# One block for the context's last rows, the heads and the attention of a perceiver layer, with statistics taken tile by tile

## The chip, the cores and the metric

The kernel runs on one core of a Trainium2 chip. The metric is the device time of one execution in microseconds; the time before is the median of three runs. The profile shows one execution with its engines: TensorE (PE, its weight loads PEld), VectorE (DVE), ScalarE (ACT), GpSimd (POOL) and SyncE (SP), which here only issues DMAs.

## The reference, cut to what matters

The input x is 32 x 32 tokens of 512 values, the context 32 batches of 257 rows of 128. A layer is a cross attention, a Mamba-like mixer with an MLP, and a mixture of experts. The change lies in the cross attention, the first 390 of 1021 us:

```python
q_hk = (hidden_q @ Wq.T).reshape(b, s, H, K)          # hidden_q: the layer norm of x; H = 16, K = 128
q_big = jnp.einsum('bshk,hkq->bshq', q_hk, w_kc_q)
kv_rope = kv_c * cos[None] + _rotate_half(kv_c) * sin[None]
q_r = jnp.einsum('bshq,hqr->bhsr', q_big, W_qr)
k_r = jnp.einsum('bld,hdr->bhlr', kv_rope, W_kr)
...
```

Softmax of q_r with k_r over the 257 rows weights the rotated context, which goes through w_kc_kv and Wo and is added to x. The kernel folds the weights of a head into small products first (N = w_kc_q and W_qr, A = Wq and N, G = w_kc_kv and Wo).

## The kernel before, in words

Every matmul of full precision is three passes of a high and a low part (`passes`, L43 to L45). High parts are copies by ScalarE, low parts subtractions by VectorE. Each engine has its own program, in order; semaphores carry the dependencies. A `Block` holds one program for each engine, and at its end all engines wait for each other.

The first block (`phase_context_tail`, L77 to L113) loads row 257 of each context batch, two small tables, the identity and the eight 128-token tiles of x (L93); VectorE rotates the rows (L101 to L105), TensorE transposes them (L113), VectorE keeps the result (L107), SP stores the rows (L96).

The second block (`phase_heads`) is the heads stage. `Norm` does the layer norm: `statistics` (L147, bn_stats of four tiles, then four bn_aggr and a sum, twice), `roots` on POOL (L144), `rows` (L162), and for each tile four transposes (`transpose_tile`, L177), a high part (L182) and a low part (L168), in three PSUM banks taken in turn. `fold_n` (L459) and `fold_a` (L470) prepare the weights of the first pair of heads between them. Then come eight passes, each of two heads. A pass has `features` for the first half of the tokens (12 matmuls of 512 columns), `fold_n` of the next pass, `turn_context` (L512, transposes of a rotated context), `features` for the second half, another turned context, `fold_a` of the next, `queries` (L501), `fold_g` (L479), and two more of each. `keep_n` (L620) and `split_a` (A_lo at L624, k_lo at L627) are VectorE's part of the folding, A_hi (L545) and k_hi (L547) ScalarE's.

POOL rotates one context batch after the other (L379 to L388, five operations), four batches to a pass. It needs the sine and cosine tables, the raw context, the tail rows of that batch in a broadcast load, and a place in x: the cosine table and one raw buffer lie in tile 3 of x, the tails in tile 2, the rotated batches in tiles 4 to 7, so SP loads the cosine table and all contexts only behind `sp.wait_ge(norm.normed, TT)` (L432), eight rows normalised. SP's queue is in order: a wait in it holds everything that is behind.

The third block (`phase_attention`) takes 32 batches in steps: `scores` (matmuls of 256 columns), maxima on VectorE (L953, L955), exponentials on ScalarE (L906), normalising on VectorE (L967) and POOL (L796), transposes (L839), the context product, and the output of a tile of tokens. The operands of its first two batches are made at the end of the heads stage (`first_columns` L646, `first_queries` L650, with the semaphores first_lo and first_q). SP loads later batches' operands from L752 and L757 on.

## Time and profile before

| | |
|---|---|
| three runs | 1024.33, 1026.26, 1026.9 us (median 1026.26) |
| the profiled execution | 1022.87 us, span 1021.1 us |
| TensorE's mean granted clock | 0.988 |
| first block, to the end of its barrier | 0 to about 7.2 us |
| heads stage | to about 137.4 us |
| attention stage | to about 390 us |

The span is what the engines' records cover; the execution's own time is 1.8 us longer. A row of the timeline gives the start in us, the time in us, the engine, the line, the operation with what it writes and reads, how many were merged into the row, and in brackets how long the engine had been idle before and what released it. A granted clock of 1.00 is 2.4 GHz, 0.50 is 1.2 GHz.

### The profile page before, as it was taken

What the parts mean: (1) busy time and instruction counts of PE and PEld (TensorE: products, weight loads), DVE (VectorE), ACT (ScalarE), POOL (GpSimd) and SP (SyncE); (2) the same over time, 40 slices, a digit from 0 to 9 for tenths busy, and PEclk for the clock granted to TensorE, in tenths of its full rate; (3) what the DMA queues carried; (4) which work ended last, traced back from release to release, by engine and by line L of the source; (5) the groups of instructions that cost most, each with busy time, mean ns of one, the idle gap of its engine ahead of it and who ended that gap; (6) DMA issues with size and microseconds to landing.
All of it is one profiled execution on the core that took longest, in us unless ns stands there. A gap on an engine that the chain in (4) does not pass through costs nothing. (4 is left out here: it accounts for less than half of the span.)

```text
span 1021.1 us, 15950 instructions
## 1 busy us (share of the span) xinstructions
PE 955.3 (94%) x5479; PEld 805.6 (79%) x5479; DVE 556.1 (54%) x1040; ACT 411.1 (40%) x954; POOL 453.3 (44%) x489
## 2 busy tenths in 40 slices
PE   4899976999999988999999999889999999999997
PEld 4677755888787866888888988677778899999997
DVE  6333468888899944444545332317968333333345
ACT  2333467677677734223432044352333122222111
POOL 1998845555576620000000302217614878993051
PEclk9999989999999999999999999999999999999999
DMA  6788702111111004422221014312023756661152
GB/s 221 231 269 264 225 13 93 35 40 42 32 37 38 27 27 130 139 83 82 82 89 36 3 59 138 102 29 81 2 85 113 262 171 235 202 225 63 42 159 99
DMA packets 79003, 109.91 MB, mean 108 GB/s; under 512 B 14224, under 2 KB 46992, under 8 KB 78928
## 3 DMA queue, kind: packets, MB, share of 16 engines
q1 hardware_dynamic: 66288, 82.18, 25.9%
q10 hardware_dynamic: 10080, 18.35, 5.0%
q0 software_dynamic: 2560, 8.39, 2.5%
q8 instruction: 45, 0.74, 0.3%
q14 instruction: 30, 0.25, 0.1%
HBM read 83.13 MB, written 25.77 MB: 107 GB/s over the span
## 5 line engine op out<-in xcount | busy, mean ns | idle before, releaser
L43 PE MATMUL psum<-second_xT_hi,second_w_hi 128*128 128x512 f32 x272 | 107.6, 396 | 7.0 <-DVE second_w_lo L1259 3.8
L45 PE MATMUL psum<-second_xT_hi,second_w_lo 128*128 128x512 f32 x272 | 106.6, 392 | 0.0
L44 PE MATMUL psum<-second_xT_lo,second_w_hi 128*128 128x512 f32 x272 | 106.5, 392 | 0.0
L1152 POOL TENSOR_TENSOR all_x<-all_x,mlp_raw 128x512 f32<-128x512 f32 x8 | 10.0, 1290 | 174.7 <-DVE all_x L1654 174.7
L2172 ACT ACTIVATE moe_s<-psum 128x352 f32<-128x352 f32 x39 | 18.1, 465 | 151.0 <-PE psum L45 151.0
L43 PEld LDWEIGHTS psum<-second_xT_hi,second_w_hi 128*128 128x128 f32 x272 | 51.4, 189 | 20.0 <-DVE second_w_lo L1259 5.3
L2238 DVE TENSOR_TENSOR moe_hT_lo<-psum,moe_hT_hi 128x384 fp32r<-128x384 f32 x39 | 21.8, 558 | 79.1 <-ACT moe_hT_hi L2178 79.1
L1609 ACT ACTIVATE mlp_s<-psum,mlp_side 128x512 f32<-128x512 f32 x32 | 21.8, 682 | 100.3 <-PE psum L45 100.3
L43 PE MATMUL psum<-moe_w_hi,moe_tT_hi 128*128 x184 | 61.3, 333 | 0.0
L1654 DVE TENSOR_TENSOR all_x<-all_x,psum 128x512 f32<-128x512 f32 x64 | 43.8, 687 | 31.7 <-PE psum L45 31.2
L45 PEld LDWEIGHTS psum<-second_xT_hi,second_w_lo 128*128 128x128 f32 x272 | 51.4, 189 | 11.0
L44 PEld LDWEIGHTS psum<-second_xT_lo,second_w_hi 128*128 128x128 f32 x272 | 51.5, 189 | 10.5
L45 PE MATMUL psum<-moe_w_hi,moe_tT_lo 128*128 x184 | 59.1, 321 | 0.0
L44 PE MATMUL psum<-moe_w_lo,moe_tT_hi 128*128 x184 | 58.9, 320 | 0.0
L43 PE MATMUL psum<-q_G_hi,att_cT_hi 128*128 128x512 f32 x128 | 53.3, 416 | 0.9 <-DVE all_x L985 0.9
L2019 POOL TENSOR_TENSOR moe_w_lo<-far_raw,moe_w_hi 128x1408 fp32r<-128x1408 f32 x16 | 51.6, 3226 | 0.0
L44 PE MATMUL psum<-q_G_lo,att_cT_hi 128*128 128x512 f32 x128 | 50.7, 396 | 0.0
L43 PE MATMUL psum<-moe_w_hi,moe_hT_hi 128*128 (+3 forms) x117 | 48.4, 414 | 2.2 <-DVE moe_hT_lo L2238 2.2
L1648 DVE TENSOR_TENSOR mix_wo_lo<-mlp_s,mix_wo_hi 128x512 fp32r<-128x512 f32 x32 | 22.1, 690 | 51.5 <-ACT mix_wo_hi L1615 51.5
L45 PE MATMUL psum<-mix_wo_hi,mix_wo_lo 128*128 128x512 f32 x128 | 49.9, 390 | 0.0
L43 PE MATMUL psum<-mix_wo_hi 128*128 128x512 f32 x128 | 49.9, 390 | 0.0
L44 PE MATMUL psum<-mix_wo_lo,mix_wo_hi 128*128 128x512 f32 x128 | 49.8, 389 | 0.0
(341 smaller groups left out, 2887.0 us busy)
## 6 DMA issues: line engine op xcount, KB each, us to landing
kv_all<-all_x ACTq DMA_DIRECT2D x28, 256.0 KB, 4.1
far_raw<-in_eg SPq DMA_DIRECT2D x10, 704.0 KB, 4.6
far_raw<-in_eu SPq DMA_DIRECT2D x10, 704.0 KB, 4.6
slot_rows<-mix_W SPq DMA_DIRECT2D x23, 256.0 KB, 5.9
slot_out<-far_rows ACTq DMA_DIRECT2D x23, 256.0 KB, 2.4
far_raw<-in_ed SPq DMA_DIRECT2D x10, 512.0 KB, 4.1
far_rows<-slot_rows ACTq DMA_DIRECT2D x19, 256.0 KB, 2.9
second_raw<-in_w_feat SPq DMA_DIRECT2D x18, 256.0 KB, 3.3
```

The source lines that it names most:

```text
L43: e.matmul(out, hi_l, hi_r, start=first, stop=False)
L44: e.matmul(out, hi_l, lo_r, start=False, stop=False)
L45: return e.matmul(out, lo_l, hi_r, start=False, stop=last)
L1152: pool.tensor_tensor(g["x"][:, t, :], g["x"][:, t, :], b2, ALU.add).then_inc(x_plus, 1)
L1609: act.activation(s1[:, m % 2, :], psum[:, UP + m % 4, :], ACT.Gelu_apprx_tanh, bias=side[:, p, c:c + 1]).then_inc(act_ok, 1)
L1648: v.tensor_tensor(h_lo[:, c, half * HALF:(half + 1) * HALF], s1[:, m % 2, :], h_hi[:, c, half * HALF:(half + 1) * HALF].bitcast(F32), ALU. ...
L1654: v.tensor_tensor(x[:, t, :], x[:, t, :], psum[:, DN + t % 4, :], ALU.add).then_inc(dn_ok, 1)
L2019: pool.tensor_tensor(w1_lo[:, u, i, :, :], raw1[:, i, :, :], w1_hi[:, u, i, :, :].bitcast(F32), ALU.subtract).then_inc(w_ok, 1)
L2172: act.activation(s[:], psum[:, GB + j % 2, 0:FE], ACT.Silu).then_inc(s_ok, 1)
L2238: v.tensor_tensor(hT_lo[:], psum[:, HB, 0:NC * P].rearrange("p (c k) -> p c k", k=P), hT_hi[:].bitcast(F32), ALU.subtract).then_inc(hlo_ok, 1)
```

## The change

The three blocks become one. `phase_heads` and `phase_attention` return their programs, and `phase_opening` puts one behind the other on every engine; the work of the first block goes to the front of the heads' programs, with its small tiles in the raw context buffers and the rotated row in `rows`. Where a block's end had ordered things, waits on semaphores stand: POOL and SP wait for `heads.rot` of all 32 batches, TensorE for first_q and first_lo of each of the first two batches and for all of G, ScalarE for kvT_ok, VectorE for kept. `statistics` is split into `tile_statistics` and `moments`. VectorE takes them as tiles land and normalises the first rows before the second half's statistics are complete. TensorE transposes tiles 4 to 6 between the groups of the first half's features and tile 7 behind them. SP issues the first two contexts and the tail store before it waits, the cosine table once four rows are normalised instead of eight; POOL waits for one more normalised row before each of its first four batches.

```diff
-def phase_context_tail(nc, d, g):
...
-    def statistics(self, v):
-        for half in range(2):
-            tiles = range(half * TT // 2, (half + 1) * TT // 2)
-            for t in tiles:
-                v.wait_ge(self.loaded[t], 16)
-                v.bn_stats(self.stats[:, t, :], self.g["x"][:, t, :]).then_inc(self.stat_done, 1)
-            for t in tiles:
-                v.wait_ge(self.stat_done, t + 1)
-                v.bn_aggr(self.mv[:, t, :], self.stats[:, t, :]).then_inc(self.aggr, 1)
-            v.wait_ge(self.aggr, (half + 1) * TT // 2)
-            these = slice(tiles[0], tiles[-1] + 1)
-            v.tensor_scalar(self.var[:, these, 0], self.mv[:, these, 1], EPS, None, ALU.add).then_inc(self.var_done, 1)
+    def tile_statistics(self, v, t):
+        v.wait_ge(self.loaded[t], 16)
+        v.bn_stats(self.stats[:, t, :], self.g["x"][:, t, :]).then_inc(self.stat_done, 1)
+
+    def moments(self, v, half):
+        tiles = range(half * TT // 2, (half + 1) * TT // 2)
+        for t in tiles:
+            v.wait_ge(self.stat_done, t + 1)
+            v.bn_aggr(self.mv[:, t, :], self.stats[:, t, :]).then_inc(self.aggr, 1)
+        v.wait_ge(self.aggr, (half + 1) * TT // 2)
+        these = slice(tiles[0], tiles[-1] + 1)
+        v.tensor_scalar(self.var[:, these, 0], self.mv[:, these, 1], EPS, None, ALU.add).then_inc(self.var_done, 1)
 
...
+
+        row, cosr, sinr, t2 = (raw[0:B, i, j, :] for i in range(2) for j in range(2))
+        turned = rows[0:B, 0:P]
...
         g["kv_out"] = kv_out
-        block = ctx.enter_context(nc.Block())
-
-        @block.gpsimd
-        def _(pool):
+        loaded, rotated, turned_T, kept = n.sem("loaded"), n.sem("rotated"), n.sem("turned_T"), n.sem("kept")
+
+        def gpsimd(pool):
             norm.roots(pool)
             pool.wait_ge(tables, 32)
+            pool.wait_ge(g["tail_stored"], 16)
             for b in range(B):
                 src, kvr = raws[b % RAW], kvx[:, b % KVB, 0, :, :]
                 pool.wait_ge(raw_in[b % RAW], 16 * (b // RAW + 1))
 
                 wait(pool, kv_out[b % KVB], 16 * (b // KVB))
+                if b < KVB:
+
+                    pool.wait_ge(norm.normed, TT - KVB + b + 1)
 
                 wait(pool, rot_sum, b)
                 pool.tensor_tensor(kvr, src, cosb[:], ALU.mult).then_inc(rot_mid, 1)
...
                     load_context(b + RAW)
                 if b % 2 == 1 and b + 3 < B:
                     load_tails((b + 3) // 2)
+            sp.dma_start(row, d["ctx"][:, L - 1, :]).then_inc(loaded, 16)
+            sp.dma_start(cosr, d["cos_last"]).then_inc(loaded, 16)
+            sp.dma_start(sinr, d["sin_last"]).then_inc(loaded, 16)
+            sp.dma_start(ident[:], d["ident"]).then_inc(loaded, 16)
+            for t in range(TT):
+                sp.dma_start(x[:, t, :], d["x"][t * P:(t + 1) * P, :]).then_inc(g["x_loaded"][t], 16)
             load_n(0)
             load_a(0)
+            sp.wait_ge(rotated, 4)
+            sp.dma_start(d["tail_rows"][:, :], turned).then_inc(g["tail_stored"], 16)
             sp.dma_start(sinb, d["sin_main"]).then_inc(tables, 16)
+            load_context(0)
+            load_context(1)
             load_g(0)
+            sp.wait_ge(norm.normed, TT - KVB)
+            sp.dma_start(cosb, d["cos_main"]).then_inc(tables, 16)
             sp.wait_ge(g["tail_stored"], 16)
+            load_tails(0)
+            load_context(2)
             load_n(1)
+            load_tails(1)
             load_a(1)
-            sp.wait_ge(norm.normed, TT)
-            sp.dma_start(cosb, d["cos_main"]).then_inc(tables, 16)
-            load_context(0)
-            load_tails(0)
-            load_context(1)
-            load_context(2)
-            load_tails(1)
             for p in range(NP):
                 contexts(BPP * p)
                 if p + 2 < NP:
...
                 for c in range(DC):
                     m = passes(pe, psum[:, RB + half, :], A_hi[:, c, :], A_lo[:, c, :], xT_hi[:, c, cols], xT_lo[:, c, cols],
                                c == 0, c == DC - 1)
+                    if p == 0 and half == 0 and c < DC - 1:
+                        norm.transpose_tile(pe, TT // NHALF + c)
                 m.then_inc(r_ready, 1)
+                if p == 0 and half == 0:
+                    norm.transpose_tile(pe, TT - 1)
 
             def queries(p, half):
                 pe.wait_ge(k_kept, p + 1)
...
                 for c in range(2):
                     m = pe.transpose(psum[:, KT, c * P:(c + 1) * P], kvx[:, b % KVB, 0, c, :], ident[:])
                 m.then_inc(kvT_ready, 1)
-            for t in range(3):
+            pe.wait_ge(rotated, 4)
+            pe.transpose(psum[:, NB, 0:B], turned, ident[0:B, 0:B]).then_inc(turned_T, 1)
+            pe.wait_ge(kept, 1)
+            for t in range(2):
                 norm.transpose_tile(pe, t)
             fold_n(0)
+            norm.transpose_tile(pe, 2)
+            fold_a(0)
             norm.transpose_tile(pe, 3)
-            norm.transpose_tile(pe, 4)
-            fold_a(0)
-            for t in range(5, TT):
-                norm.transpose_tile(pe, t)
             for p in range(NP):
                 features(p, 0)
                 if p + 1 < NP:
...
                 nb, h, half = HALF // S, 2 * p, 1 - half
                 act.activation(q[:, half * nb:(half + 1) * nb, h * S:(h + 1) * S],
                                psum[:, XB, :].rearrange("p (b s) -> p b s", s=S), ACT.Copy).then_inc(q_kept[0], 1)
-            for t in range(5):
+            for t in range(3):
                 norm.high_part(act, t)
             keep_a(0)
-            for t in range(5, TT):
+            for t in range(3, TT):
                 norm.high_part(act, t)
             for p in range(NP):
                 keep_features(p, 0)
...
                 v.wait_ge(first_q_hi, s + 1)
                 v.tensor_tensor(q_lo[:, s, :], q[:, place_of(s), :], q_hi[:, s, :].bitcast(F32), ALU.subtract).then_inc(first_q, 1)
 
-            norm.statistics(v)
-            v.wait_ge(g["tail_stored"], 16)
+            v.wait_ge(loaded, 64)
+            v.tensor_tensor(turned, row, cosr, ALU.mult).then_inc(rotated, 1)
+            v.tensor_tensor(t2[:, 0:64], row[:, 64:128], sinr[:, 0:64], ALU.mult).then_inc(rotated, 1)
+            v.tensor_tensor(t2[:, 64:128], row[:, 0:64], sinr[:, 64:128], ALU.mult).then_inc(rotated, 1)
+            v.wait_ge(rotated, 3)
+            v.tensor_tensor(turned, turned, t2, ALU.add).then_inc(rotated, 1)
             for t in range(4):
-                norm.rows(v, t)
-            for t in range(2):
-                norm.low_part(v, t)
-                norm.rows(v, 4 + t)
+                norm.tile_statistics(v, t)
+            norm.moments(v, 0)
+            v.wait_ge(turned_T, 1)
+            v.tensor_copy(g["tailT"][:], psum[:, NB, 0:B]).then_inc(kept, 1)
+            norm.tile_statistics(v, 4)
+            norm.tile_statistics(v, 5)
+            norm.rows(v, 0)
+            norm.rows(v, 1)
+            norm.tile_statistics(v, 6)
+            norm.tile_statistics(v, 7)
+            norm.moments(v, 1)
+            norm.rows(v, 2)
+            norm.rows(v, 3)
+            norm.low_part(v, 0)
+            norm.low_part(v, 1)
             keep_n(0)
-            for t in range(2, 4):
-                norm.low_part(v, t)
-                norm.rows(v, 4 + t)
-            norm.low_part(v, 4)
+            norm.low_part(v, 2)
+            norm.rows(v, 4)
+            norm.low_part(v, 3)
+            norm.rows(v, 5)
             split_a(0)
-            for t in range(5, TT):
+            norm.rows(v, 6)
+            norm.rows(v, 7)
+            for t in range(4, TT):
                 norm.low_part(v, t)
             for p in range(NP):
...
-        def _(sp):
+        def sync(sp):
             kv_out = g["kv_out"]
             KVB = len(kv_out)
+
+
+            sp.wait_ge(heads.rot, B)
...
                 of = pr(b)[:, 2:4, :]
                 pool.tensor_tensor(of, of, pair(scale, b, 1).unsqueeze(2).to_broadcast([P, 2, LM]), ALU.mult).then_inc(pr_far_ok, 1)
 
+            pool.wait_ge(heads.rot, B)
             pool.memset(g["power"][:], -0.5).then_inc(power_set, 1)
...
                     columns_lo(s + 2)
                     queries_lo(s + 2)
 
-        @block.tensor
-        def _(pe):
+        def tensor(pe):
             def scores(b):
                 p = b % 2
-                wait(pe, q_ok, b + 1 - DONE)
-                wait(pe, kvT_ok, b + 1 - DONE)
+                if b < DONE:
+                    pe.wait_ge(heads.first_q, b + 1)
+                    pe.wait_ge(heads.first_lo, b + 1)
+                else:
+                    pe.wait_ge(q_ok, b + 1 - DONE)
+                    pe.wait_ge(kvT_ok, b + 1 - DONE)
                 if b - 2 in EARLY:
 
...
 
-            def output(t, heads):
-                if heads[0] == 0:
+            def output(t, heads_now):
+                if heads_now[0] == 0:
+                    if t == 0:
+                        pe.wait_ge(heads.g_kept, H)
                     pe.wait_ge(c_ok, BPT * (t + 1))
...
+            act.wait_ge(heads.kvT_ok, B)
             for s in range(B + 2 + BPT):
...
+            v.wait_ge(heads.kept, 1)
...
+    made.gpsimd, made.sync, made.tensor, made.scalar, made.vector = gpsimd, sync, tensor, scalar, vector
+    return made
+
+
+def phase_opening(nc, heads, attention):
+    with nc.Block() as block:
+
+        @block.gpsimd
+        def _(pool):
+            heads.gpsimd(pool)
+            attention.gpsimd(pool)
+
+        @block.sync
+        def _(sp):
+            heads.sync(sp)
...
```

## Rows read from the trace of the kernel before

**Rows 1.** The page, part 1: busy time, share, instructions of each engine.
```profile
PE 955.3 (94%) x5479; PEld 805.6 (79%) x5479; DVE 556.1 (54%) x1040; ACT 411.1 (40%) x954; POOL 453.3 (44%) x489
```

**Rows 2.** Table by stage: stretch, length, busy of each engine, PEclk, DMA share, GB/s.
```profile
39.42:122.46 83.04, 81.10 (x460) 61.31 (x458) 31.46 (x54) 33.52 (x72) 75.71 (x127) 1.00 0.84 257
137.44:260.00 122.56, 108.02 (x617) 93.33 (x618) 103.84 (x224) 86.36 (x287) 66.74 (x74) 0.96 0.16 48
```

**Rows 3.** Timeline of the opening, VectorE: the first four statistics.
```profile
7.23 2.47 DVE L152 BATCH_NORM_STATS2 all_stats<-all_x 128x6 f32<-128x512 f32 x4 [1.82 <-PEq L79]
```

**Rows 4.** Line L93 (min/median/max); DMA issues from 9.65 to 10 us, time to landing.
```profile
L93 SPq DMA_DIRECT2D all_x<-in_x x8: 432/432/437, 2.6 to 5.9; - x8
DMA to landing us min/median/max: 2.7/4.3/5.2
...
heads_wkr<-in_wkrT SPq DMA_DIRECT2D x1, 64.0 KB, 5.0
```

**Rows 5.** Timeline of the opening: POOL's root, VectorE, ScalarE.
```profile
10.34 1.05 POOL L144 TENSOR_TENSOR heads_rstd<-heads_var,heads_power 128x4 f32<-128x4 f32 x1 [3.04 <-DVE heads_var L158]
...
12.97 1.91 DVE L162 TENSOR_SCALAR queries_q<-all_x,heads_mv,heads_rstd 128x512 f32<-128x512 f32 x4
...
18.38 0.29 DVE L620 COPY queries_q<-psum 128x128 f32<-128x128 f32 x1 [0.83 <-PE psum L459]
...
19.64 0.68 DVE L168 TENSOR_TENSOR first_xT_lo<-psum,first_xT_hi 128x512 fp32r<-128x512 f32 x1
...
20.99 0.60 ACT L545 ACTIVATE heads_A_hi<-psum 128x512 fp32r<-128x512 f32 x1 [1.08 <-PE psum L470]
21.49 0.30 ACT L547 ACTIVATE heads_k_hi<-heads_wkr 128x128 fp32r<-128x128 f32 x1
21.62 0.69 DVE L624 TENSOR_TENSOR heads_A_lo<-psum,heads_A_hi 128x512 fp32r<-128x512 f32 x1 [0.25 <-ACT heads_A_hi L545]
```

**Rows 6.** Timeline of the opening, TensorE.
```profile
13.57 2.82 PE L177 MATMUL psum<-all_ident,queries_q 128*128 128x128 f32 x12 [8.39 <-DVE queries_q L162]
16.19 2.15 PE L459 MATMUL psum<-queries_q,heads_kcqT 128*128 128x64 f32 x12
18.18 1.04 PE L177 MATMUL psum<-all_ident,queries_q 128*128 128x128 f32 x8
19.06 1.90 PE L470 MATMUL psum<-queries_q,heads_wq 128*128 128x64 f32 x16
```

**Rows 7.** Timeline of the first pass, TensorE and POOL's first rotation.
```profile
22.37 0.50 PE L43 MATMUL psum<-first_xT_hi,heads_A_hi 128*128 128x512 f32 x1
...
25.28 1.45 PE L459 MATMUL psum<-queries_q,heads_kcqT 128*128 128x64 f32 x12
...
26.20 0.73 POOL L379 TENSOR_TENSOR all_x<-heads_raw,all_x 128x256 f32<-128x256 f32 x1 [11.73 <-DMA heads_raw<-in_ctx]
...
29.47 0.44 PE L512 MATMUL psum<-all_ident,all_x 128*128 128x128 f32 x2 [2.75 <-POOL all_x L388]
...
29.66 0.48 PE L43 MATMUL psum<-first_xT_hi,heads_A_hi 128*128 128x512 f32 x1
...
39.42 0.48 PE L43 MATMUL psum<-first_xT_hi,heads_A_hi 128*128 128x512 f32 x1
```

**Rows 8.** Timeline of the seam between heads and attention, VectorE and TensorE.
```profile
135.23 0.69 DVE L650 TENSOR_TENSOR first_xT_hi<-queries_q,first_xT_hi 128x512 fp32r<-128x512 f32 x1 [0.76 <-ACT first_xT_hi L574]
...
136.44 0.68 DVE L650 TENSOR_TENSOR first_xT_hi<-queries_q,first_xT_hi 128x512 fp32r<-128x512 f32 x1
...
137.44 0.55 PE L43 MATMUL psum<-first_xT_hi 128*128 128x256 f32 x1 [2.11 <-PEq L327]
...
139.10 0.69 DVE L953 TENSOR_REDUCE att_low<-psum 128x2 f32<-128x512 f32 x1 [1.99 <-PE psum L45]
```

**Rows 9.** Table by stage, two microseconds behind the seam (columns as in rows 2).
```profile
138.00:140.00 2.00, 2.00 (x11) 2.00 (x11) 0.86 (x2) 0.00 (x0) 0.00 (x0) 0.50 0.47 130
```

**Rows 10.** Line L218, VectorE's normalising rows in the attention stage: duration ns min/median/max.
```profile
L218 DVE TENSOR_SCALAR queries_q<-all_x,att_mv,att_rstd x14: 535/542/1509, 260.2 to 376.5; 128x512 f32<-128x512 f32 x14
```

More of the change, by code:

```diff
@@ L865, in _ @@
                 t, k = divmod(s - BPT - 2, BPT)
-                heads = [OH * k + i for i in range(OH)]
+                these = [OH * k + i for i in range(OH)]
                 if s - 1 in EARLY:
@@ L2422, in build @@
         g["x_back"] = n.sem("x_back")
-        phase_context_tail(nc, d, g)
         edge = ExitStack()
```

88 lines of the change are left out of this document (34 added, 54 removed).

## The prediction

> **What bounds the kernel now.** I read the page first: TensorE is busy for 94% of the span, no other engine for more than 54% [rows 1], so the time moves only where TensorE waits or where its work is longer than it need be. The table by stage comes next [rows 2]. In the steady part of the heads stage, 39.42 to 122.46 us, TensorE is busy for 81.10 of 83.04 us: six passes at 13.84 us each, bound by it; nothing outside can shorten them, and everything ahead of them shifts them whole. In the attention stage VectorE is at 104 of 123 us and TensorE at 108, each waiting for the other inside a step; I take that chain too as one that shifts with its start. So what the change is worth is read at three places: the opening up to the first features, the gap in the first pass, and the seam between heads and attention.
>
> The opening, in the timeline: VectorE could take statistics as tiles land, but stands 1.82 us for the first block's end and begins at 7.23 [rows 3], though tile 0 was in by 5.3 (issued at 2.6, 2.7 to landing) and the last of the eight by 11.1 (5.9 and 5.2) [rows 4]. It does all eight before the first row is normalised at 12.97 [rows 5], and TensorE's first transposes start at 13.57 [rows 6]. Features begin at 22.37. Then POOL, which has waited for context data, starts to rotate only at 26.20, and TensorE stands 2.75 us until 29.47 [rows 7]. At the seam, TensorE is idle 2.11 us up to 137.44 [rows 8].
>
> **The change, part by part.** *Removed barrier after the tail rows, statistics by tile.* TensorE's 32-column transpose, VectorE's copy and the stored tail rows stay. The fourth tile lands near 8.1 (tiles 3 and 4, issued near 4.2, take the median 4.3). Statistics cost 2.47/4 = 0.62 us, so half a set is done at 8.75. Before, POOL's root started 0.64 us after the fourth (9.70 to 10.34) and took 1.05 [rows 3, 5]: now it ends at 10.45. VectorE meanwhile does the copy (some 0.2) and tiles 4 and 5 (1.24) and reaches the first row at about 10.75. Before, the transposes began 0.6 us behind the first row's start (12.97 to 13.57); now at 11.35, 2.2 us earlier.
>
> *What eats most of that.* Two tiles of transposes at 2.82/12 = 0.235 us each go to 13.2, and fold_n takes 2.15 [rows 6]: 15.3. (The later eight take 1.04, 0.13 each; the first ones are slow in both kernels, and I leave them so.) The weights are in by then: they queue behind x, and the last of them (wkr) landed 5.0 us after its issue at 9.65 [rows 4], and their order behind x is kept. VectorE from 11.3: row 1 (1.91/4 = 0.48), tiles 6 and 7 (1.24), aggregates (some 0.5, as between 9.70 and POOL's start), rows 2 and 3 (0.96, so at 14.5 four rows are out), two low parts (1.36) = 15.8; keep_n, 0.29, waits behind them: 16.1. fold_a 1.90: 18.0. ScalarE: A_hi 0.60, k_hi 0.30, high part of tile 3 0.60: 19.5. VectorE: low 3 0.68, row 5 0.48, A_lo 0.69 [rows 5]: 21.4, and with a hand-off 21.5, against 22.37. The late step is the order: A_lo sits behind low 3, which needs a copy that ScalarE makes after A_hi.
>
> *Port.* POOL's rotation starts at about 18 instead of 26.20: sine table and two contexts are issued early, cosine at about 14.5 once four rows are out; with some 3 us to landing, an estimate from the 2.7 to 5.2 seen [rows 4], that is 18. It runs beside rows 5 to 7 and k_lo on VectorE. The trace has such normalising rows beside POOL in the attention stage: 0.542 us median, 1.509 at most [rows 10], so a meeting costs 0 to 0.97. Only row 5 is ahead of A_lo; I take 0.35, nearer the median, as POOL has only part of the time left in an operation of 0.73 [rows 7]. Features then start at 21.85. What the page of the Trainium skill "SBUF — State Buffer", section "Who interferes with whom", says speaks against the change: POOL and a two-port VectorE operation exclude each other for the whole instruction. By it every one of the four would be held up; the 0.73 us and the maximum agree with blocking, the median with mostly missing it.
>
> *Four tiles' transposes between the features.* The first half took 2.91 us from 22.37 to 25.28 [rows 7]; four tiles at 1.04/2 = 0.52 [rows 6] add 2.1. So fold_n starts at 26.85, ends (1.45) at 28.3. The last tile's high and low parts, 0.60 + 0.68 behind its transposes, end at about 28.2: just hidden. The context is long turned by POOL, so the 2.75 us wait is gone. The second half starts 0.2 us behind the turning (29.47 to 29.66 before), at 28.5 instead of 29.66. The 2.1 us of transposes are not saved, only moved (before, they ran before 22.37 while TensorE waited for rows). From there to the next pass took 9.76 us; in a steady pass it is 13.84 less the 2.91, 1.45 and 0.2 ahead of it, 9.3. The difference is more waiting for POOL, which goes too; I take 9.5: 38.0 against 39.42. **Opening: 1.4 us.** From both sides: 0 if what is hidden above shows (each 0.1 us that the last low part is later than 28.3 delays the turning), 2.2 if the whole lead of the first transposes is kept.
>
> *SP's queue.* The tail store, sine, two contexts and the first G weights now stand ahead of a wait for four rows (to 14.5), behind which cosine, tails, load_n(1) and load_a(1) queue. load_n(1) waits for fold_n(0) at 15.3 anyway: nothing. POOL's new waits, one normalised row for each of its first four contexts, end by 22.6, while a context takes it 75.71/24 = 3.15 us [rows 2], so the third starts no sooner than 24: hidden. Later POOL, started 8 us sooner, is ahead and waits for TensorE's turning and the stores; it has 12.6 us of work in a pass of 13.84: hidden. If that cover went, POOL's rotation would again be late at each turning.
>
> *No barrier at the seam.* Scores of the first batch wait for first_q, ready at 135.23 + 0.69 = 135.92. VectorE still owes the second (136.44 + 0.68 = 137.12). The first maxima, at 139.10 [rows 8], need half the scores: at 2.4 GHz about 0.95 us (an estimate, 1.66 halved with some latency left), 136.9. So they start at 137.15: 1.95 us earlier. At the lower of its two levels (granted clock 0.50, 1.2 GHz, at 138 to 140 [rows 9]; the 1.66 us from 137.44 to 139.10 are at that) 135.96 + 1.66 = 137.6: 1.5. I take 1.95: TensorE's gap falls from 2.1 to 0.6. Column and row loads follow POOL's last rotation and come earlier; nothing waited for them: nothing. ScalarE's wait for its own last copy: nothing.
>
> **Sum** against the profiled execution (1022.87, span 1021.1): 1.4 + 1.95 = 3.35 us, 1019.5. That execution lies 3.4 us under the median of the runs shown (1026.26); off the median, 1022.9. About 0.3% (3.1 us) is what a measurement can tell from no change, so this stands right at that edge.
>
> **Rivals.** *The clock in the opening.* TensorE has little to do from 18.5 to 21.85, and at the seam a gap of 2.1 us was followed by clock 0.50. If it falls here, the first features (2.91 us) run at up to twice the time: some 1.4 us, and the opening is worth nothing. Total 1.95: 1024.3. For it: the seam. Against: the gap from 26.73 to 29.47 in the kernel before had the same risk, and in this trace did not pay.
>
> *The port.* All four meetings at 0.97, no misses: features 0.6 later than I have it and the low parts of tiles 4 to 7 about 1.0, no longer hidden. 3.35 - 1.6 = 1.75: 1024.5. What "SBUF — State Buffer" of the Trainium skill states would make this the likely outcome.
>
> *Better.* Before, executions other than this one pay for the clock at the 2.75 us wait and at the seam; the new kernel has neither. Another 1.4 plus 0.7 us: 1020.8.
>
> *Slower.* The clock in the attention stage, 137 to 394 us. Mean granted clock 0.96 over its first 122.56 us [rows 2] means 0.04 x 2 x 122.56 = 9.8 us at the lower level, worth 4.9 us. It decides from 3.35 us of extra loss, 1.7 times as much as before; at 2.3 times, 6.5 us more, it ends 3.2 us slower: 1029.5. Nothing in the rows makes it likelier than its opposite.
>
> **How the numbers follow.** Forecast 0.48 (own range 1022.0 to 1024), better 0.20, clock 0.18, port 0.10, slower 0.04. Faster by over 0.3%, below 1023.2: the better case and 0.33 of the forecast's, 0.53; slower 0.04; the rest, 0.43, within. Range: from 1019.6 to 1025.6 takes in the better case with its error and both lesser ones.
>
> **What would show it.** Right: first normalised row at 10.5 to 11, first features at 21.2 to 22.2 with transposes between them, POOL's first rotation near 18, no wait of TensorE for POOL in the first pass, second pass at 37.5 to 38.5, first maxima less than 15 us behind the last pass's start (before 139.10 - 122.46 = 16.64). Wrong: rows or A_lo of 1 us or more on VectorE; clock 0.50 between 20 and 26; a new wait for low parts ahead of fold_g or the second half; POOL short of context data; an attention stage that is not as long as before.

## The result, and the profile after

| | before | after |
|---|---|---|
| median of 21 runs each, one chip | 1025.5 us (1022.96 to 1028.0) | 1023.46 us (1020.47 to 1024.99) |
| profiled execution | 1022.87 us, span 1021.1 | 1020.47 us, span 1018.6 |
| mean granted clock of TensorE | 0.988 | 0.991 |

The ratio of the two is 0.9975, with an interval of 0.9967 to 0.9984: 0.25% faster, clear of no change, but just inside the 0.3% named in the prediction. The forecast was 1022.9. The time was about right, but not for the reasons given: one of the two terms held, the other brought nothing that the runs can tell from zero, and in this profile less than nothing.

The page of the changed kernel hardly differs from [rows 1]; as there, the answer is not in the shares.

```profile
PE 957.3 (94%) x5479; PEld 807.3 (79%) x5479; DVE 557.9 (55%) x1040; ACT 411.3 (40%) x954; POOL 452.7 (44%) x489
```

The timeline of VectorE in the opening (start, busy time, engine, line, and in brackets the idle time before and what ended it) answers to [rows 3, 5]. L109 is the statistics, L122 a normalised row, L128 a low part, L599 and L602 the low parts of A and k.

```profile
5.81 2.78 DVE L109 BATCH_NORM_STATS2 all_stats<-all_x 128x6 f32<-128x512 f32 x4 [0.95 <-DMA all_x<-in_x]
...
10.44 0.99 DVE L122 TENSOR_SCALAR queries_q<-all_x,heads_mv,heads_rstd 128x512 f32<-128x512 f32 x2
...
16.01 0.29 DVE L595 COPY queries_q<-psum 128x128 f32<-128x128 f32 x1 [0.81 <-PE psum L431]
...
21.65 0.69 DVE L128 TENSOR_TENSOR first_xT_lo<-psum,first_xT_hi 128x512 fp32r<-128x512 f32 x1 [3.02 <-ACT first_xT_hi L142]
22.26 0.54 DVE L122 TENSOR_SCALAR queries_q<-all_x,heads_mv,heads_rstd 128x512 f32<-128x512 f32 x1
22.71 0.68 DVE L599 TENSOR_TENSOR heads_A_lo<-psum,heads_A_hi 128x512 fp32r<-128x512 f32 x1
23.31 0.49 DVE L602 TENSOR_TENSOR heads_k_lo<-heads_wkr,heads_k_hi 128x128 fp32r<-128x128 f32 x1
```

Statistics start 1.4 us earlier, and the first row is out 2.5 us earlier (10.44 against 12.97). That part of the plan works. TensorE's timeline in the same stretch answers to [rows 6, 7]. L137 is a tile's transposes, L431 fold_n, L442 fold_a, L43 to L45 the features, L488 the turning.

```profile
11.11 1.94 PE L137 MATMUL psum<-all_ident,queries_q 128*128 128x128 f32 x8 [5.89 <-DVE queries_q L122]
13.15 2.82 PE L431 MATMUL psum<-queries_q,heads_kcqT 128*128 128x64 f32 x12
15.77 1.06 PE L137 MATMUL psum<-all_ident,queries_q 128*128 128x128 f32 x4
16.62 3.51 PE L442 MATMUL psum<-queries_q,heads_wq 128*128 128x64 f32 x16
19.93 1.06 PE L137 MATMUL psum<-all_ident,queries_q 128*128 128x128 f32 x4
23.45 0.79 PE L43 MATMUL psum<-first_xT_hi,heads_A_hi 128*128 128x512 f32 x1 [2.47 <-DVE heads_A_lo L599]
...
24.90 1.05 PE L137 MATMUL psum<-all_ident,queries_q 128*128 128x128 f32 x4
...
27.60 0.48 PE L43 MATMUL psum<-first_xT_hi,heads_A_hi 128*128 128x512 f32 x1
...
29.96 1.45 PE L431 MATMUL psum<-queries_q,heads_kcqT 128*128 128x64 f32 x12
31.63 0.41 PE L488 MATMUL psum<-all_ident,all_x 128*128 128x128 f32 x2 [0.22 <-DVE first_xT_lo L128]
31.80 0.48 PE L43 MATMUL psum<-first_xT_hi,heads_A_hi 128*128 128x512 f32 x1
...
41.57 0.48 PE L43 MATMUL psum<-first_xT_hi,heads_A_hi 128*128 128x512 f32 x1
```

Compare line by line with [rows 6, 7]. The transposes start 2.46 us earlier (11.11 against 13.57). Then fold_n takes 2.82 us, not 2.15; fold_a takes 3.51, not 1.90; and behind a 2.47 us wait the first features still run at half pace: the first three take 1.45 us (23.45 to 24.90), the third three 0.78 (27.60 to 28.38). The same kernel has fold_n at 1.45 once the pace is full (29.96). So TensorE runs at the lower of its two levels (1.2 GHz) until about 27.45; before, it reached 2.4 GHz at about 17.7. The second pass starts at 41.57 instead of 39.42: in this profile the opening costs 2.15 us instead of gaining 1.4. One caution on reading: the column of the granted clock says 1.00 for this whole stretch, and for 13.5 to 17.7 us of the kernel before too; I take it that no record of the clock had come yet. The pace of like instructions tells what the column doesn't: 16 records of 64 columns in 3.51 us or in 1.90.

The seam (VectorE's and TensorE's timelines) answers to [rows 8]:

```profile
138.22 0.39 PE L43 MATMUL psum<-first_xT_hi 128*128 128x256 f32 x1 [0.64 <-DVE first_xT_hi L625]
...
138.68 0.68 DVE L625 TENSOR_TENSOR first_xT_hi<-queries_q,first_xT_hi 128x512 fp32r<-128x512 f32 x1
...
139.31 0.69 DVE L954 TENSOR_REDUCE att_low<-psum 128x2 f32<-128x512 f32 x1
```

TensorE waits 0.64 us instead of 2.11, its scores follow each other at full pace, and the first maxima start 14.60 us behind the last pass (139.31 - 124.71), before 16.64: 2.04 us, forecast 1.95. Of these, 1.47 are the shorter wait (2.11 - 0.64). The other 0.57 are the pace of the scores: from the first of them to the maxima it is 1.09 us (138.22 to 139.31) instead of the 1.66 at the lower clock in [rows 8, 9].

The table by stage (length; busy time of TensorE, its weight loads, VectorE, ScalarE, POOL; granted clock, DMA share, GB/s) shows the rest, against [rows 2]:

```profile
41.57:124.71 83.14, 81.03 (x459) 61.32 (x458) 32.13 (x54) 33.51 (x72) 71.71 (x120) 1.00 0.87 255
124.71:139.31 14.60, 11.95 (x60) 8.11 (x59) 6.64 (x12) 6.76 (x14) 9.41 (x17) 1.00 0.36 96
139.31:260.00 120.69, 105.61 (x620) 91.34 (x619) 104.91 (x230) 87.56 (x292) 66.73 (x73) 0.99 0.16 47
```

The six steady passes take 83.14 us, as before (83.04). So at the first maxima the changed kernel is 0.21 us behind the old one (139.31 against 139.10), and yet its profiled execution is 2.5 us shorter: it makes this up behind the seam (879.3 us from there to the end against 882.0), where the change touches nothing. The attention stage has a granted clock of 0.99 where [rows 2] had 0.96. Is that an effect? A second profile of the changed kernel, below, on another chip, took 884.8 us from the first maxima to the end (1024.6 - 139.78), and the other kernels, which share this code, from 880.8 to 896.2. So one execution against another says nothing here about 2.5 us. Hence every kernel below was timed in turn with the kernel before, and the profiles are read for places, not for totals.

### The profile page after: what moved, and what is told of

Read it like the earlier page. It is cut to its first block and busy times, and to the rows that moved or that the text cites. A ratio compares the mean times of both kernels' runs of the same rounds, so it can differ in the third digit from the quotient of the medians.

```text
span 1018.6 us, 15933 instructions
## 1 busy us (share of the span) xinstructions
PE 957.3 (94%) x5479; PEld 807.3 (79%) x5479; DVE 557.9 (55%) x1040; ACT 411.3 (40%) x954; POOL 452.7 (44%) x489
## 5 line engine op out<-in xcount | busy, mean ns | idle before, releaser
L43 PE MATMUL psum<-second_xT_hi,second_w_hi 128*128 128x512 f32 x272 | 107.4, 395 | 6.9 <-DVE second_w_lo L1293 3.8
L45 PE MATMUL psum<-second_xT_hi,second_w_lo 128*128 128x512 f32 x272 | 106.6, 392 | 0.0
L43 PEld LDWEIGHTS psum<-second_xT_hi,second_w_hi 128*128 128x128 f32 x272 | 51.2, 188 | 19.9 <-DVE second_w_lo L1293 5.3
L43 PE MATMUL psum<-moe_w_hi,moe_tT_hi 128*128 x184 | 61.3, 333 | 0.0
L45 PEld LDWEIGHTS psum<-second_xT_hi,second_w_lo 128*128 128x128 f32 x272 | 51.3, 189 | 10.9
L45 PE MATMUL psum<-moe_w_hi,moe_tT_lo 128*128 x184 | 59.1, 321 | 0.0
L43 PE MATMUL psum<-q_G_hi,att_cT_hi 128*128 128x512 f32 x128 | 53.4, 417 | 0.9 <-DVE all_x L986 0.9
L43 PE MATMUL psum<-moe_w_hi,moe_hT_hi 128*128 (+3 forms) x117 | 48.9, 418 | 2.2 <-DVE moe_hT_lo L2272 2.2
L45 PE MATMUL psum<-mix_wo_hi,mix_wo_lo 128*128 128x512 f32 x128 | 49.9, 390 | 0.0
L43 PE MATMUL psum<-mix_wo_hi 128*128 128x512 f32 x128 | 49.9, 390 | 0.0
```

The costliest lines, as they stand in the source:

```text
L43: e.matmul(out, hi_l, hi_r, start=first, stop=False)
L45: return e.matmul(out, lo_l, hi_r, start=False, stop=last)
```

## The experiments

My theory after the result: the seam gives 2 us always; in the opening the low clock lasts longer and eats the lead; and the transposes between the first features are paid in full, while TensorE stands idle ahead of them. Rivals: the port; the order on VectorE; the contexts; and that the low clock came by chance, or from too little work on TensorE before 11 us.

"Against before" is the ratio to the kernel before, timed in turn with it on the same chip, with its 95% interval. The kernels ran on three chips: two_blocks, seam_only, placed_before and busy on one (kernel before 1024.8 us); after_again, warm, placed_warm and before_warm on a second (1031.41); the other four on a third (1025.5).

### Each half of the change alone

**two_blocks**: the changed kernel with the barrier at the seam put back.

```
         def _(pool):
             heads.gpsimd(pool)
+    with nc.Block() as block:
+        @block.gpsimd
+        def _(pool):
             attention.gpsimd(pool)
...
```

> The changed kernel, but with the end of a block put back between the heads and the attention stage. Theory: the seam is worth 2.0 us (last pass to first maxima 16.64 us before, 14.60 after), so this kernel is 2.0 us slower than the changed one, and its first maxima come 16.6 us behind the start of the last pass. Against the kernel before it then shows the opening alone: on my theory the opening is worth nothing on the average (in the one profile the second pass started 2.15 us later than before), 0 +/- 1 us. Rival, that the opening is worth its predicted 1.4 us and the seam loses elsewhere: 1.4 us faster than before.

**seam_only**: the opening of before, but heads and attention in one block. It keeps before's own block for the tail rows, statistics in a row, late contexts, and all transposes ahead of the features.

```
+        phase_context_tail(nc, d, g)
...
+            for h in range(2):
+                for t in range(4):
+                    norm.tile_statistics(v, 4 * h + t)
+                norm.moments(v, h)
...
```

> The opening of the kernel before (its first block and barrier, all statistics first, all transposes ahead of the features, contexts loaded late), with heads and attention in one block. Theory: 2.0 us faster than before, all of it at the seam, 14.6 us from the last pass to the first maxima, and as fast as the changed kernel within 0.7 us. Rival, that the opening brings its 1.4 us: this kernel is 1.4 us slower than the changed one.

Measured: two_blocks 1025.39 us, against before 1.0015 (0.9995 to 1.0034); seam_only 1023.87 us, 0.9993 (0.9975 to 1.0012). At the seam each does what it should. The timeline of two_blocks there:

```profile
142.00 0.35 PE L43 MATMUL psum<-first_xT_hi 128*128 128x256 f32 x1 [2.27 <-PEq L1023]
...
143.40 0.69 DVE L954 TENSOR_REDUCE att_low<-psum 128x2 f32<-128x512 f32 x1 [1.88 <-PE psum L45]
```

With its last pass at 126.86 that is 16.54 us, the old length and the old wait for the block's end; seam_only has 14.56 (124.78 to 139.34). The 2 us belong to the barrier. The opening alone brings nothing that shows: between 0.5 us gained and 3.5 lost, which leaves out the 1.4 us forecast. Its one profile was worse still, since the statistics stood twice more for tiles of x (0.54 and 0.63 us): first transposes at 12.26 instead of 11.11, second pass at 43.04. But seam_only did not bring its 2 us in the median; its interval, 2.6 us gained to 1.2 lost, just holds them, and no run shows what took the rest. Its profile shows something else, on the opening of before. TensorE's timeline, and the table over the microseconds behind the turning:

```profile
29.95 0.44 PE L516 MATMUL psum<-all_ident,all_x 128*128 128x128 f32 x2 [3.28 <-POOL all_x L394]
...
31.16 0.57 PE L44 MATMUL psum<-first_xT_lo,heads_A_hi 128*128 128x512 f32 x1
31.53 0.63 PE L45 MATMUL psum<-first_xT_hi,heads_A_lo 128*128 128x512 f32 x1
...
41.23 0.48 PE L43 MATMUL psum<-first_xT_hi,heads_A_hi 128*128 128x512 f32 x1
```

```profile
31.20:34.60 3.40, 3.40 (x10) 2.52 (x9) 0.00 (x0) 0.00 (x0) 3.18 (x6) 0.50 0.75 226
```

The opening of before came to its second half at 30.15, and still its second pass starts at 41.23, not 39.42: behind the wait for POOL the clock fell to 0.50 for 3.4 us. In [rows 7] it did not fall behind the same wait, there 2.75 us instead of 3.28; whether chance or that half microsecond decides, two profiles can't tell. So 39.42 was an execution that had escaped. Against 41.23 the changed kernel's 41.57 is no loss. This can't be what seam_only lacks in time, though: the kernel before has the same opening and can pay the same.

### The transposes, put back ahead of the features

**placed_before** and, on another chip, **placed_again**: the changed kernel, with all eight tiles' transposes ahead of the first features.

```
-            for t in range(2):
+            for t in range(3):
                 norm.transpose_tile(pe, t)
             fold_n(0)
-            norm.transpose_tile(pe, 2)
-            fold_a(0)
             norm.transpose_tile(pe, 3)
+            norm.transpose_tile(pe, 4)
+            fold_a(0)
+            for t in range(5, TT):
+                norm.transpose_tile(pe, t)
...
-                    if p == 0 and half == 0 and c < DC - 1:
-                        norm.transpose_tile(pe, TT // NHALF + c)
...
```

VectorE's rows, low parts and ScalarE's high parts follow in the same order.

> The changed kernel with the transposes, high and low parts in the order of before: all eight tiles ahead of the first features; statistics by tile, early contexts and the one block stay. Theory: TensorE then has work from 11.1 us on without a hole of 2.5 us ahead of the features, its slow stretch ends about where it did in the kernel before (17.7 us) or 2 us sooner, the second pass starts at 37 to 38 us, and the kernel is 1 to 2 us faster than the changed one. Rival, that moving the transposes between the features is a gain: it is 1 us slower.

> All transposes ahead of the features, once more, on the chip of the next one. Theory: 0.3 to 0.5% faster than before; second pass near 39, clock rising behind 20 us again. Rival, that the first result was the luck of that chip: 0.2% or less.

Measured: placed_before 1018.9 us, against before 0.9958 (0.994 to 0.9976); placed_again 1018.69 us in six runs, 0.9924 (0.9899 to 0.9949). On this third chip the two variants below that keep the transposes between the features had 0.9973 and 0.9985, timed in turn with it. This is the kernel that beats both; the changed kernel itself was not timed beside it on either chip. TensorE's timeline in placed_before:

```profile
14.62 2.66 PE L431 MATMUL psum<-queries_q,heads_kcqT 128*128 128x64 f32 x12
17.06 1.91 PE L137 MATMUL psum<-all_ident,queries_q 128*128 128x128 f32 x8
18.77 3.51 PE L442 MATMUL psum<-queries_q,heads_wq 128*128 128x64 f32 x16
22.08 2.77 PE L137 MATMUL psum<-all_ident,queries_q 128*128 128x128 f32 x12
24.50 0.78 PE L43 MATMUL psum<-first_xT_hi,heads_A_hi 128*128 128x512 f32 x1
...
29.25 0.48 PE L43 MATMUL psum<-first_xT_hi,heads_A_hi 128*128 128x512 f32 x1
...
38.99 0.47 PE L43 MATMUL psum<-first_xT_hi,heads_A_hi 128*128 128x512 f32 x1
```

The folds are as slow as in the changed kernel, so this is not about the clock at first. Twelve transposes stand at 22.08 where the changed kernel waits 2.47 us for A_lo. The features start 1.05 us later (24.50 against 23.45), but the second half starts 4.75 us behind them instead of 8.35. The second pass is 2.6 us earlier. Not all of that is the place of the transposes, for full pace came at 25.5 here and at 27.45 there. In placed_again the second pass starts at 36.73, because there the pace doubled inside fold_a:

```profile
18.87 2.57 PE L442 MATMUL psum<-queries_q,heads_wq 128*128 128x64 f32 x16
21.28 1.48 PE L137 MATMUL psum<-all_ident,queries_q 128*128 128x128 f32 x12
22.86 0.51 PE L43 MATMUL psum<-first_xT_hi,heads_A_hi 128*128 128x512 f32 x1
...
27.19 0.48 PE L43 MATMUL psum<-first_xT_hi,heads_A_hi 128*128 128x512 f32 x1
```

The program is the same to the letter and up to 18.9 within 0.1 us; the rise came at 20.3 in one and 25.5 in the other. The program alone doesn't settle it. This execution also prices the place alone: with all of it at full pace, the second half starts 4.33 us behind the first features (22.86 to 27.19), where busy, a variant below, with the transposes between the features and at full pace too, needs 6.46 (25.73 to 32.19). That is 2.1 us, as forecast for the transposes. Of the 3.6 us by which 8.35 exceeds 4.75, then, 2.1 are the transposes and about 1.5 the pace.

### Can work on TensorE bring the clock up earlier?

**after_again** repeats the changed kernel. **busy** gives TensorE 26 matmuls of 64 columns behind the tail rows' transpose, and 16 more ahead of the features; **warm** 26 and 12 transposes of 128 columns in the same places. **placed_warm** and **placed_warm_again** are placed_before with the first 26 transposes; **before_warm** is the kernel before with them. Their results are used by nothing; no part of the computation is left out.

```
+            def spin(n):
+                for i in range(n):
+                    pe.transpose(psum[:, XB, 0:P], ident[:], ident[:])
...
             pe.transpose(psum[:, NB, 0:B], turned, ident[0:B, 0:B]).then_inc(turned_T, 1)
+            spin(26)
             pe.wait_ge(kept, 1)
```

> The changed kernel itself, once more, for a second profile and beside the next kernels on one chip. Theory: where TensorE's clock rises is set by what TensorE does in the opening, so again not before the first features: fold_n at 2.8, fold_a at 3.5 us, second pass at 41 to 43 us, 0.2 to 0.3% faster than before. Rival, that the late rise (27.5 us) was chance: the rise near 17 to 21 us, second pass at 38 to 39.

> The changed kernel with TensorE kept at work in its two waits: 26 matmuls of the identity (64 columns) into an unused bank behind the small transpose, and 16 behind the transposes of tile 3; their results are not used. Theory: in the changed kernel TensorE is slow until 27 us (fold_n 2.82, fold_a 3.51 us against 1.45 and 1.90 when fast), so with the extra matmuls fold_n takes 1.5, fold_a 1.9, features start by 20.5 instead of 23.45, the second pass by 37.5 instead of 41.57, and the kernel is 2.5 to 4 us faster than the changed one. Rival, that VectorE's order (A_lo behind low part 3 and row 5) sets the opening: less than 0.7 us, features still at 22 to 23.

> The changed kernel with 26 transposes of the identity (128 columns each, 0.21 us when slow) into an unused bank behind the small transpose, and 12 more behind the transposes of tile 3; results not used. With 64-column matmuls the extra work overran the wait by 5 us (each counted double) and the clock still rose only at 18.1. Theory: 26 x 0.21 = 5.5 us fit into the 6 us wait, the clock rises by 11 to 15 us, fold_a takes 1.9 us, features start near 21, the second pass at 37 to 38.5, and the kernel is 2 to 4 us faster than the changed one. Rival, that the order on VectorE sets the opening whatever the clock: less than 0.7 us. Second rival, that the clock does not rise by such work: no change, rise at 25 us or later.

> The changed kernel with all transposes ahead of the features (which was 0.4% faster than before), and 26 transposes of the identity behind the small transpose. Theory: its second pass, at 38.99 us in the profile with the clock rising only at 25.5, comes at 34.5 to 36 us with the clock up by 15; 2 to 3 us faster than without, 0.6 to 0.7% faster than before. Rival, that there rows and low parts on VectorE now set the start of the features: second pass not before 37, less than 1 us.

> All transposes ahead of the features and 26 transposes of the identity in the first wait, once more. Theory: second pass at 34 to 35, 4.5 us ahead of the kernel without them, and a ratio to before of 0.992 to 0.995. Rival, that what the extra work gains in the opening is given back at later low stretches: no faster than without it.

> The kernel before with 26 transposes of the identity ahead of the first tile's, in the 6 us in which TensorE waits for it. Theory: the kernel before has its clock up at 17.6 us already (two profiles), so only the first transposes and fold_n gain, 1.3 us at most, and the wait for POOL behind the first features takes it back, since POOL starts by eight normalised rows, which VectorE sets: 0 to 0.5 us faster. Rival, that the clock in the opening is worth as much here as in the changed kernel: 2 us or more.

| | median, us | against before | full pace from, us | features, us | second pass, us |
|---|---|---|---|---|---|
| after_again | 1029.24 | 0.9989 (0.9962 to 1.0017) | 27.95 | 23.62 | 41.80 |
| busy | 1024.14 | 1.0025 (0.9995 to 1.0054) | 18.13 | 25.73 | 41.72 |
| warm | 1025.59 | 0.9949 (0.9917 to 0.998) | 8.63, low again 15.5 to 22.3 | 22.59 | 38.63 |
| placed_warm | 1024.1 | 0.993 (0.99 to 0.996) | 8.71 | 20.37 | 34.24 |
| placed_warm_again | 1018.77 | 0.993 (0.9908 to 0.9952) | 8.36, low again 12 to 25 | 25.03 | 39.33 |
| before_warm | 1028.51 | 0.9962 (0.9934 to 0.999) | 11.86 | 20.83 | 39.81 |

after_again has the low folds again (2.82 and 3.51) and the second pass at 41.80: the changed kernel's profile was no accident of one execution. The columns behind the ratio are read from the one profile of each; full pace is where the spacing of like records halves. busy was a bad tool. The trace has two records for each of its matmuls, 0.22 us each:

```profile
5.14 11.36 PE L427 MATMUL psum<-all_ident 128*128 128x64 f32 x52
16.29 1.91 PE L137 MATMUL psum<-all_ident,queries_q 128*128 128x128 f32 x8
18.00 1.51 PE L435 MATMUL psum<-queries_q,heads_kcqT 128*128 128x64 f32 x12
...
25.73 0.47 PE L43 MATMUL psum<-first_xT_hi,heads_A_hi 128*128 128x512 f32 x1
...
32.19 0.48 PE L43 MATMUL psum<-first_xT_hi,heads_A_hi 128*128 128x512 f32 x1
```

They overran the wait by 5 us, and TensorE, never idle from 5.14, came to full pace only at about 18. Its median says little: seven of its twelve runs lie between 1021.2 and 1024.4 us and five between 1029.1 and 1033.5, and no run shows why. The 26 transposes took 4.77 us, and the pace doubled at 8.63. In warm:

```profile
5.07 4.77 PE L427 MATMUL psum<-all_ident 128*128 128x128 f32 x26
11.19 1.06 PE L137 MATMUL psum<-all_ident,queries_q 128*128 128x128 f32 x8 [1.34 <-DVE queries_q L122]
13.22 1.55 PE L435 MATMUL psum<-queries_q,heads_kcqT 128*128 128x64 f32 x12 [0.97 <-DMA queries_q<-in_wqr]
...
15.62 3.65 PE L446 MATMUL psum<-queries_q,heads_wq 128*128 128x64 f32 x16 [0.40 <-DVE queries_q L601]
```

fold_n is fast, but it now waits for its weights, and behind three short waits the clock falls (0.50 from 15.5 to 22.3): fold_a is at 3.65 again. In the two executions of the same program that placed_warm and placed_warm_again are, one stays at full clock from 8.71 on (fold_a 1.97, second pass 34.24), the other falls at 12, behind a wait for the first row of 2.02 us, where the first had waited 1.69:

```profile
12.00:14.00 2.00, 1.67 (x8) 1.27 (x6) 1.97 (x9) 0.89 (x2) 0.19 (x1) 0.50 1.08 354
```

and in the other, placed_warm:

```profile
14.00:18.00 4.00, 3.84 (x33) 3.61 (x34) 4.00 (x10) 1.68 (x3) 0.95 (x1) 1.00 1.06 313
```

So early work can bring a second pass at 34.24, 7.3 us ahead of the changed kernel's, but not reliably. Timed beside each other on one chip, placed_again and placed_warm_again had 1018.69 and 1018.77 us: over the executions the extra work bought nothing that six runs of each can tell, and a gain of 2 us would be within their intervals. With the transposes between the features it may have helped (0.9949 against 0.9989 for after_again on one chip, but the intervals overlap); in the kernel before it did, by 0.9962, an interval without 1. before_warm has the first features at 20.83, and yet its second pass at 39.81: it waits 3.38 us for POOL, as seam_only waited 3.28, and the clock falls behind that wait (28.9 to 32.3).

### The order on VectorE, and the contexts

**a_lo_first**: A_lo and k_lo move ahead of the low part of tile 3.

```
+            split_a(0)
             norm.low_part(v, 3)
             norm.rows(v, 5)
-            split_a(0)
```

> The changed kernel with VectorE taking A_lo and k_lo ahead of low part 3 and row 5. Theory: A_hi is ready at 20.8, so A_lo comes at 20.8 instead of 22.71 and the features then wait for low part 3 alone (21.65 + 0.69): they start at 22.4 to 22.6 instead of 23.45, second pass at 40.5, and the kernel is 1 us faster than the changed one; the late clock stays. Rival, that the order is what matters most in the opening: features at 21.5, second pass at 39 or earlier.

**late_contexts**: cosine table, contexts and tail rows are issued where the kernel before issued them, behind eight normalised rows (the sine table stands ahead of them in all kernels).

```
-            load_context(0)
-            load_context(1)
             load_g(0)
...
+            sp.wait_ge(norm.normed, TT)
             sp.dma_start(cosb, d["cos_main"]).then_inc(tables, 16)
+            load_context(0)
...
```

> The changed kernel with SP's queue in the order of before: contexts, cosine table and tails only behind eight normalised rows. Theory: the early loads do not pay in the changed kernel, since its first turning comes only at 31.6 us: with eight rows out at 25.0, POOL starts at 28.5, has its first context at 32, and TensorE waits 0.3 to 1 us for it; 0.3 to 1 us slower than the changed kernel. Rival, that they are worth the 2.75 us wait of before: second pass at 44 or later.

Measured: a_lo_first 1022.99 us, against before 0.9973 (0.996 to 0.9986); late_contexts 1023.14 us, 0.9985 (0.9967 to 1.0003). VectorE in a_lo_first:

```profile
20.78 0.69 DVE L599 TENSOR_TENSOR heads_A_lo<-psum,heads_A_hi 128x512 fp32r<-128x512 f32 x1 [2.16 <-ACT heads_A_hi L521]
21.39 0.77 DVE L602 TENSOR_TENSOR heads_k_lo<-heads_wkr,heads_k_hi 128x128 fp32r<-128x128 f32 x1
22.08 0.68 DVE L128 TENSOR_TENSOR first_xT_lo<-psum,first_xT_hi 128x512 fp32r<-128x512 f32 x1
```

A_lo is 1.9 us earlier, but now the low part of tile 3 is last, and features start at 22.91 instead of 23.45, the second pass at 40.82 instead of 41.57. The order costs 0.5 to 0.8 us, as the prediction had it ("the late step is the order"), but it is the small part. In time it can't be told from the changed kernel (0.9973 here, 0.9975 there). In late_contexts POOL's first rotation waits for its data until 27.59 (18.81 in the changed kernel):

```profile
27.59 0.72 POOL L345 TENSOR_TENSOR all_x<-heads_raw,all_x 128x256 f32<-128x256 f32 x1 [12.38 <-DMA heads_raw<-in_ctx]
```

and the second pass starts at 41.98, 0.2 to 0.4 us later than in the two profiles of the changed kernel. The wait of 0.3 to 1 us for POOL that I had expected is not there. With TensorE this slow, its turning comes at 32.28, and the late context was ready at 30.83. The early contexts can pay only where TensorE would be there first, as in placed_before, where it turns at 29.11; that kernel was not run with late contexts.

## Why the prediction was right, and where it was not

**The start of the opening: right.** Half the statistics were done at 8.59 (forecast 8.75), POOL's root at 10.28 (10.45), the first row at 10.44 (10.75), the first transposes at 11.11 (11.35), POOL's first rotation at 18.81 (about 18). keep_n ended at 16.30 for 16.1, but by luck: VectorE was through with its low parts at 15.20, not 15.8, and then stood 0.81 us for the slow fold_n. TensorE had no wait for POOL left in the first pass, SP's queue held up nothing that mattered, and the last low part, "just hidden", showed 0.22 us.

**The step that failed** is in *What eats most of that*: "fold_n takes 2.15", "fold_a 1.90: 18.0", and "the first ones are slow in both kernels, and I leave them so". The slow transposes in [rows 6] were not a property of those instructions. They were TensorE at its lower level, and the 2.15 of fold_n was a fold in whose midst it rose. I carried that rise over to work that starts 2.5 us earlier. It did not come along: fold_n took 2.82 us and fold_a 3.51, fold_a ended at 20.13 instead of 18.0, features started at 23.45 instead of 21.85, and six of the first features and two tiles' transposes ran at half pace (features to second half 8.35 us instead of 6.65). With 9.77 instead of 9.5 behind the second half, that is the whole 3.6 us from 38.0 to 41.57. The rival "the clock in the opening" named the right resource and the right worth of the opening (nothing), but had the clock fall in the gap; here it had not risen yet.

**The size of the opening's term.** Forecast 1.4 gained. In profiles, 2.15 lost against [rows 7], or 0.3 lost against seam_only, whose opening is before's with the clock fallen behind POOL's wait; timed alone, 0.5 gained to 3.5 lost. The bound "0 if what is hidden above shows" was not low enough.

**What I had in hand and did not use.** The prediction has fold_a end at 18.0 and features start at 21.85, and puts 2.1 us of transposes behind them. It calls these "not saved, only moved". They were moved out of a wait and onto the path. The price is 2.1 us at full pace (6.46 against 4.33 from the first features to the second half), less the 1.05 us by which they delay the features when they stand ahead. The rest of the 2.6 us by which placed_before has its second pass earlier, about 1.5, is the earlier full pace. On one chip placed_again had 1018.69 us against 1022.99 for a_lo_first; its profile, with full pace from 20.3, is 4.1 us ahead at the second pass (36.73 against 40.82). Whether having the transposes ahead also brings full pace earlier, these few profiles can't say.

**The port: a term of 0.35 that did not occur.** Row 5 took 0.54, the cost of one alone: at 22.26 POOL had ended its first context (22.02) and stood 0.90 us, waiting for this very row. That wait, which I had called hidden, was on nobody's path either. What met POOL was k_lo (0.49 and, in a_lo_first, 0.77, against 0.28 in placed_before) and rows 6 and 7 (1.28 for two, against 0.99 for two alone). In the changed kernel none of these 0.2 to 0.3 us was on the path. In a_lo_first k_lo's was: low part 3, on which the features waited, had its high part at 21.61 and started only behind k_lo at 22.08, some 0.4 us later. And in placed_again one row took 0.94 us beside POOL (0.54 alone), so meetings of the size that I had put in do occur. A_lo took its usual 0.69 with an operation of POOL in progress. The Trainium skill's page "SBUF — State Buffer", section "Who interferes with whom", has a VectorE operation with two inputs in SBUF contend with a POOL operation that reads SBUF, and one with at most one input there, outside the two-port modes, not. The trace agrees: k_lo reads two inputs from SBUF (0.77 us for 0.28), A_lo reads one of its two from PSUM (0.69 us as ever).

**The seam: right**, 2.04 for 1.95, with the barrier put back 16.54 again, and in its parts: TensorE's wait fell to 0.64 (forecast 0.6), the scores ran at the upper level, and the maxima followed VectorE's second low part at once (138.68 + 0.68 us). That is by profiles; in time seam_only showed 0.7 us of it. In late_contexts and placed_again it is 16.1, with a low clock inside the last pass (0.55 from 134 to 137 in the first of these) and TensorE's wait at the seam at 0.97: still no barrier.

**Better, and slower.** Neither happened by its mechanism. "Better" was right that other executions of before's opening pay for the clock at the wait for POOL (seam_only and before_warm do), but the new opening still pays for it too, ahead of and in its first features. The attention stage had no more low clock than before (0.99 over 139 to 260 us).

**The sum.** 3.35 forecast; by the ratio 2.6 measured, by the medians 2.0. The seam gives 2.04 in the profiles, the opening nothing that can be told from zero. That 1023.46 lies only 0.6 us from the forecast is partly luck: the kernel before had a median of 1025.5 us beside it, 0.8 us under the 1026.26 that I had subtracted from. The interval of the ratio (1.6 to 3.4 us) would even take in 3.35; it is the profiles and two_blocks, not the total, that show the term of the opening wrong. A second timing of the changed kernel, after_again, gave 0.9989 (0.9962 to 1.0017), which holds a gain of 2 us and none. What stays open: the halves timed alone sum to 1.0008, which is 3.4 us above the 0.9975 of the whole; their intervals, some 2 us each way, and two chips stand between these. Open too is what makes the clock rise and fall at different times in executions of one program.

## What to carry to other kernels

When work is moved, ask at which clock each of its instructions ran: rows of one instruction at two durations, a factor of two apart, are one cost at two levels, and the level does not travel with the instruction. Before moving work off the path to a first result, look at whether the engine is idle ahead of that result: transposes placed in the 2.5 us wait for A_lo delayed the features by 1.05 us and took 2.1 us off the way from there to the second half. The barrier between two blocks could be priced from the first work that waited behind it, here 2 us, of which 1.5 are the wait and 0.6 the lower pace behind it; that was the surest part of the change.

## What the runs showed of the hardware

TensorE stayed at its lower level through 13 us without a wait (busy, 5.14 to 18; 26 matmuls of 64 columns and eight transposes) and through 16 us with one wait of 2.47 us in it (the changed kernel, 11.11 to 27.45). With back-to-back transposes of 128 columns from 5.07 (warm), 5.20 (placed_warm) and 5.10 (placed_warm_again) full pace was there at 8.63, 8.71 and 8.36. With the same program, the rise came at 20.3 or 25.5 (placed_again, placed_before), and a spell of clock 0.50 from 12 to 25 us was there or not (placed_warm_again, behind a wait of 2.02 us; placed_warm, behind one of 1.69). Waits of 3.3 and 3.4 us for POOL were followed by 3.4 us at 0.50 in two profiles (seam_only, before_warm), one of 2.75 us in [rows 7] was not. A VectorE operation with both inputs in SBUF took 0.49 to 0.77 us beside POOL instead of 0.28 (k_lo), one with an input in PSUM its usual 0.69 (A_lo).
